# The start of a two-layer conditioned transformer kernel, rewritten: group 0 in halves, K placed from PSUM, films on ScalarE and GpSimd, weights loaded late

## What is computed

```python
# layer 0
tp = silu(cond) @ Wt + bt          # six vectors: shift, scale, gate (attention), shift, scale, gate (MLP)
h = layernorm(x) * (1 + scale_msa) + shift_msa
h = attention(h, Wqkv, Wproj)      # 16 heads of 8, softmax over the 32 rows of a sequence
x = x + gate_msa * h
h = layernorm(x) * (1 + scale_mlp) + shift_mlp
x = x + gate_mlp * (gelu(h @ W1 + b1) @ W2 + b2)
# layer 1
h = film(rmsnorm(x), cond, film1)  # x * (1 + scale) + shift, both from cond @ w + b
x = x + softmax(Q K^T / sqrt(D)) V @ proj + proj_b     # one head of 128
h = film(rmsnorm(x), cond, film2)
x = x + gelu(h @ mlp_w1 + b) @ mlp_w2 + b
```

## Time and profile before

| | us |
|---|---|
| median of 3 runs | 259.19 (258.96 to 259.65) |
| the profiled execution | 258.97 |
| its span in the trace | 257.1 |
| TensorE busy | 236.4 |
| VectorE busy | 163.9 |
| ScalarE busy | 154.9 |
| GpSimd busy | 151.1 |

### The profile page before, as it was taken

The page is one execution under the profiler, slowest core; times in us unless marked ns, Lnnn a source line. Parts: engine busy times, 40 slices in busy tenths (PEclk is TensorE's granted clock), DMA queues, the critical chain, the costliest instruction groups (busy, mean ns, idle before and its releaser), DMA issues.

```text
span 257.1 us, 9816 instructions
## 1 busy us (share of the span) xinstructions
PE 236.4 (92%) x3696; PEld 176.7 (69%) x3696; DVE 163.9 (64%) x510; ACT 154.9 (60%) x394; POOL 151.1 (59%) x161
## 2 busy tenths in 40 slices
PE   0588878999999998999999999999999999999995
PEld 0556556868778775687766669767775666777775
DVE  4868997879999999374454455378888444542002
ACT  2368566658668658925566545888757665444440
POOL 7442543855857768776666766797783545553110
PEclk9999999999999999999999999999999999999999
DMA  6964324443433443340000000000000011101112
GB/s 214 311 244 110 101 72 107 108 126 109 115 118 114 126 122 97 112 147 1 3 0 0 0 0 0 1 3 4 0 3 3 0 45 42 41 1 40 41 43 82
DMA packets 17451, 18.01 MB, mean 70 GB/s; under 512 B 2320, under 2 KB 13072, under 8 KB 17296
## 3 DMA queue, kind: packets, MB, share of 16 engines
q1 hardware_dynamic: 16848, 15.67, 21.6%
q10 hardware_dynamic: 576, 1.98, 2.3%
HBM read 11.48 MB, written 4.59 MB: 63 GB/s over the span
## 4 chain that ended last, share of the span: by engine, by line
PE 77%; DVE 7%; issue 5%; ACT 3%; POOL 3%; DMA 3%; SPq 1%; ACTq 0%; POOLq 0%; DVEq 0%
PE bank L1146 22%; PE bank L962 10%; PE pair L962 10%; PE bank L938 5%; PE bank L1036 5%; PE pair L1006 4%; PE bank L1057 3%; PE bank L1018 2%; PE pair L1159 2%; PE bank L1153 2%; PE bank L1184 2%; ACT xhat L770 2%; PE bank L1006 2%; DMA X<-x 2%; PE bank L986 2%
## 5 line engine op out<-in xcount | busy, mean ns | idle before, releaser
L770 ACT ACTIVATE xhat<-X,shift,rstd 128x128 f32 (+1 forms) x96 | 40.3, 486 | 50.7 <-POOL shift L332 50.6
L1146 PE MATMUL bank<-W,Kx 128*128 128x128 f32 x512 | 59.6, 275 | 0.0
L1146 PEld LDWEIGHTS bank<-W,Kx 128*128 128x128 f32 x512 | 58.5, 192 | 1.0 <-issue 1.0
L343 POOL TENSOR_TENSOR h<-hA,B 128x512 f32<-128x512 f32 x32 | 33.6, 1049 | 34.4 <-DVE hA L505 34.1
L505 DVE TENSOR_TENSOR hA<-bank,A 128x512 f32<-128x512 f32 x32 | 21.8, 681 | 32.3 <-PE bank L938 17.0
L962 PE MATMUL bank<-h,W 128*128 128x512 f32 x62 | 32.0, 597 | 0.1
L351 POOL TENSOR_TENSOR Ss<-Sc,smax 128x512 f32<-128x512 f32 x16 | 16.8, 1051 | 25.9 <-DVE smax L531 25.9
L330 POOL TENSOR_TENSOR rstd<-v_sb,minus_half 128x4 f32<-128x4 f32 x24 | 24.6, 1026 | 11.6 <-DVE v_sb L490 6.5
L962 PE MATMUL pair<-h,W 128*128 128x512 f32 x62 | 29.4, 592 | 0.0
L938 PEld LDWEIGHTS bank<-ident,xhat 128*128 128x128 f32 x128 | 15.9, 146 | 16.6 <-issue 12.2
L825 ACT ACTIVATE Kx<-bank,col 128x512 f32<-128x512 f32 x32 | 21.7, 678 | 8.1 <-PE bank L962 8.1
(11 more groups left out here) (132 smaller groups left out, 452.0 us busy)
## 6 DMA issues: line engine op xcount, KB each, us to landing
values_scratch<-Vs SPq DMA_DIRECT2D x8, 288.0 KB, 2.2
Vx<-values_scratch SPq DMA_DIRECT2D x32, 72.0 KB, 2.1
gate<-gates_scratch SPq DMA_DIRECT2D x32, 64.0 KB, 2.2
gate<-gates_scratch SPq DMA_DIRECT2D x16, 128.0 KB, 2.6
out<-X SPq DMA_DIRECT2D x7, 256.0 KB, 2.3
Kx<-Ks SPq DMA_DIRECT2D x24, 64.0 KB, 1.9
W<-weights ACTq DMA_DIRECT2D x1, 1152.5 KB, 6.2
X<-x SPq DMA_DIRECT2D x4, 256.0 KB, 6.8
```

The lines of the kernel that those rows point to most:

```text
L343: pool.tensor_tensor(by_seq(h[:, p, :]), by_seq(hA[:, p, :]), B[:, seqs(gg)].unsqueeze(2).broadcast_to([P, GB, L]), ALU.add).then_inc(h_re ...
L770: last = act.activation(xhat[:, p, P * t:P * (t + 1)], X[:, x_tile(gg, t), :], ACT.Identity, bias=shift[:, p, t:t + 1], scale=rstd[:, p, t ...
L1146: last = pe.matmul(y[t // 2][:, P * t:P * (t + 1)], gT[:, p, n, P * t:P * (t + 1)], w(f"W2_{phase // 2}", n), start=(n == 0), stop=(n == N ...
```

## The change

Weights are laid out anew (`Wqkv` right behind `Wt`, layer 1's V weight stored transposed, `v1T`), and the loads are split and moved: `Wt` in two pieces around the rows of group 1, `Wqkv` alone from ScalarE's queue, then the films and projections. The rest of `x` (groups 4 to 7) is loaded behind the first spread of V. The MLP weights of layer 0 are loaded in group 5 of attention 0, those of layer 1 in the first group of MLP 0.

```diff
@@ sync
-            lo, hi = W_AT["Wt"][0], W_AT["Wproj"][0]
-            sp.dma_start(W[:, lo:hi], weights[:, lo:hi]).then_inc(wt_in, 16)
-            for g in range(1, 4):
+            lo, mid, hi = W_AT["Wt"][0], W_AT["Wt"][0] + 2 * D, W_AT["Wqkv"][0]
+            sp.dma_start(W[:, lo:mid], weights[:, lo:mid]).then_inc(wt01_in, 16)
+            sp.dma_start(X[:, TG:2 * TG, :], xv[:, TG:2 * TG, :]).then_inc(x_in[1], 16)
+            sp.dma_start(W[:, mid:hi], weights[:, mid:hi]).then_inc(wt_in, 16)
+            for g in range(2, 4):
                 sp.dma_start(X[:, TG * g:TG * (g + 1), :], xv[:, TG * g:TG * (g + 1), :]).then_inc(x_in[g], 16)
-            sp.dma_start(X[:, 4 * TG:, :], xv[:, 4 * TG:, :]).then_inc(x_in[4], 16)
...
                 sp.dma_start(values_d[p], Vs[:, p, :]).then_inc(v_stored[p], 16)
+                if g == 1:
+                    store_gates()
                 sp.wait_ge(v_stored[p], 16 * (g // 2 + 1))
...
-            sp.wait_ge(gate_ready, 1)
-            for b in range(TB):
-                sp.dma_start(gates_d[b].rearrange("i t d -> t i d"),
-                             gate_b[b:NB:TB, :].rearrange("t (i d) -> t i d", i=2)).then_inc(gates_stored, 16)
-            sp.wait_ge(zeros_ready, 1)
+            sp.wait_ge(zeros_ready, 2)
             spread_v(0, 0)
-            sp.wait_ge(gates_stored, 16 * TB)
-            spread_gates(0, 0, NG)
+            sp.dma_start(X[:, 4 * TG:, :], xv[:, 4 * TG:, :]).then_inc(x_in[4], 16)
             for g in range(1, NG):
                 spread_v(g, g % 2)
                 if g < NG - 1:
                     spread_k(g + 1, (g + 1) % 2)
+                if g == 1:
+                    sp.wait_ge(gates_stored, 16 * TB)
+                    spread_gates(0, 0, NG)
...
@@ scalar
+                if isinstance(g, int) and g == NG - 3:
+                    lo, hi = W_AT["W1_0"][0], W_AT["W1_1"][0]
+                    act.dma_start(W[:, lo:hi], weights[:, lo:hi]).then_inc(wmlp_in, 16)
...
+                        lo = W_AT["W1_1"][0]
+                        act.dma_start(W[:, lo:], weights[:, lo:]).then_inc(wmlp1_in, 16)
```

```diff
@@ vector
+            def place_k_low(half):
+                dve.wait_ge(k2_ready, half + 1)
+                at, k_ps = slice(GN // 2 * half, GN // 2 * (half + 1)), bank[5][:, GN // 2:GN] if half == 0 else bank[6][:, 0:GN // 2]
                 for r in (0, 1):
-                    last = dve.tensor_scalar(Kx[:, g, r, :], Ks[:, g, :], r_mask[:, r:r + 1], None, ALU.mult)
+                    last = dve.tensor_scalar(Kx[:, 0, r, at], k_ps, c("bk"), r_mask[:, r:r + 1], ALU.add, ALU.mult)
                 last.then_inc(k_placed, 1)
+            def apply_first(gg):
+                dve.wait_ge(pool_chain, gg + 2)
+                for t in range(TG):
+                    last = dve.tensor_scalar(xhat[:, gg, P * t:P * (t + 1)], X[:, x_tile(gg, t), :].rearrange("p t d -> p (t d)"),
+                                             mk[:, gg, t:t + 1], rstd[:, gg, t:t + 1], ALU.add, ALU.mult)
...
+            apply_first(0)
+            modulate_half(0)
+            dve.tensor_tensor(B[:, 0:NB], bank[5][:, 0:NB], t_mul[:, :], ALU.add).then_inc(ab_ready, 1)
+            modulate_half(1)
@@ scalar
+            def place_k_high(half):
+                for r in (2, 3):
+                    last = act.activation(Kx[:, 0, r, at], bank[3][:, at], ACT.Identity, bias=r_bias[:, r:r + 1],
+                                          scale=r_mask[:, r:r + 1])
@@ gpsimd
+            pool.tensor_tensor(gate_b[:, :], xg[:, 0, 2 * NB:4 * NB], row[:, 0:2, :].rearrange("p i d -> p (i d)"),
+                               ALU.add).then_inc(gate_ready, 1)
+            film0_rest()
             add_shift(1, 1)
+            subtract_max(0, 0)
             power(2, 0)
@@ tensor
+            for n in range(24):
+                pe.transpose(bank[7][:, 0:P], ident[:, :], ident[:, :])
...
+            pe.wait_ge(ab_ready, 1)
+            first_qk(0)
+            values0(0, 0)
...
+            scores0(0, 0)
+            rows_T(1, 1)
+            first_qk(1)
+            film1()
+            keys0(1, 1)
```

More of the change, by code:

```diff
@@ new lines, in _ @@
+            link(last)
+            dve.tensor_scalar(ag0[:, :], c("g1"), one_plus[:, 0:1], None, ALU.mult)
+            dve.tensor_scalar(ab0[:, :], c("be1"), one_plus[:, 0:1], c("bt", 0), ALU.mult, ALU.add).then_inc(cols_ready, 1)
+            dve.wait_ge(exp_c, 1)
+            link(dve.tensor_tensor(sT[:, :], eT[:, :], kind[:, 0, 2 * NG:2 * NG + 1].broadcast_to([D, NB]), ALU.add))
+            link(dve.reciprocal(eT[:, :], sT[:, :]))
+            first_stats(0)
+            dve.tensor_tensor(sT[:, :], cT[:, :], eT[:, :], ALU.mult).then_inc(y_used, 1)
@@ L689, in attention0 @@
+                update(0, g - 1, 1 - p)
                 aggregate(g + 4, p, True)
@@ L1102, in attention0 @@
                     pe.wait_ge(wmlp_in, 16)
-                if first:
-                    fold(0)
                 pe.wait_ge(v_spread[p], 16 * HQ * (k + 1))
@@ L1111, in attention0 @@
                 scores_T(g, 1)
-                if first:
-                    fold(1)
-                    pe.wait_ge(ab_ready, 3)
-                elif not last:
+                if not last:
                     project0(g - 1, 1 - p)
```

367 lines of the change are left out of this document (227 added, 140 removed).

## The result

The changed kernel takes **263.21 us** (median of 6 runs, 261.93 to 265.29); the kernel before, run on the same chip, takes 259.80 us (6 runs, 258.96 to 262.59). The ratio is 1.0141, with a 95% interval of 1.0105 to 1.0177. The change makes the kernel slower, by more than the range of the prediction allows. The profiled execution took 262.90 us, with a span of 261.1 against the 257.1 us of before.

The account below looks back on a forecast made before the run. From 60 us TensorE alone was taken to set the pace; before it VectorE was full from 20 to 40, behind the first group's latency chain. Forecast: 258.97 - 2.5 (start, after SyncE's queue) + 0.1 (weights) = 256.6 us, range 253.6 to 259.4.

Parts of the forecast that it names:

- Part 1: The first group up to its scores: first scores at 13.0 us, 5.8 before 18.83.
- Part 2: From first scores to the loop, on a full VectorE: entry at 29.6 us, 5.0 earlier, bounds 28.4 and 31.2.
- part 4: Weights moved to group 5 and the first MLP group: 0.1 us lost; late rest of X and turned V weight free.
- Part 3: SyncE's queue up to the keys of group 3: gives back gain, take-up at 48.0 instead of 50.47, 2.5 us won.
- SyncE's queue takes over: Longest row at each queue step: keys of group 3 land at 51.7, 1.2 later than before; 260.2 us, chance 0.13.
- Ports: VectorE's normalisation of group 1 meets GpSimd's gate and film operations: 1.6 us more on VectorE, 258.2 us, chance 0.13.
- Weights in the way: The load in group 5 delays V or K of the next groups: 2.6 us lost, 259.1 us, chance 0.12.
- TensorE's pace: SyncE keeps its medians, so TensorE reaches the keys of group 3 at 45.0: gain 5.4, 253.6 us, chance 0.20.

Follow-up runs that it names:

- experiment 6: Changed kernel with gates stored and first spread around V of group 0, without the 24 transposes of ident; 259.33 us, ratio 0.9980 to the kernel before.
- experiment 1: Changed kernel with the rest of x issued at the start again; 262.96 us, ratio 1.0112 to the kernel before.
- kernel 2: Changed kernel with the gates stored and first spread around V of group 0; 257.58 us, ratio 0.9887 to the kernel before.
- kernel 8: Changed kernel with gates stored and first spread around V of group 0, and gates spread two groups at a time; 257.05 us, ratio 0.9853.
- experiment 9: Changed kernel with only the gates spread two groups at a time, stores and first spread left late; 259.00 us, ratio 0.9963 to the kernel before.
- experiment 12: Kernel before with only the changed kernel's order of gate stores and spreads on SyncE; 263.95 us, ratio 1.0111 to the kernel before.
- kernel 3: Changed kernel with the rest of x at the start and gates stored and first spread around V of group 0; 256.63 us, ratio 0.9832.
- 5: Changed kernel with only the four gate stores moved behind V of group 0; 265.90 us, ratio 1.0169 to the kernel before.
- experiment 7: Changed kernel with gates stored and first spread around V of group 0, and both MLP weight loads behind the first film; 256.63 us, ratio 0.9816.
- 10: Changed kernel with gates spread two groups at a time and the rest of x at the start; 258.70 us, ratio 0.9910 to the kernel before.
- kernel 11: Changed kernel with x at the start, gates stored and first spread around V of group 0, spread two groups at a time; 255.46 us, ratio 0.9830.

## Why the prediction was wrong, step by step

**Part 1 was right.** Forecast 13.0 for the first scores, measured 13.77, within the 12.4 to 13.8 named. The terms that were off: four normalised tiles on VectorE took 1.11 us (0.28 each, not 0.2), and film 0 ended at 9.9 instead of 9.3, for which hA waited 0.60. The 24 transposes of ident took 5.32 us, to 8.3 instead of about 7.9; that the short durations hold behind them was right, and experiment 6 shows that they hold because of them.

**Part 2 failed in the changed kernel, and its sum was right.** Forecast 29.6 for the entry, bounds 28.4 to 31.2; measured 35.66. Without the late megabyte it is 30.74 (experiment 1), so the counting of VectorE's work was within 1.1 us. An entry after 31.2 was named as what would make the forecast wrong. The failed sentence is the one in part 4 that "the late rest of X (1 MB, issued near 18, used at 28) and the turned V weight (...) cost nothing, covered by part 2's VectorE work". I asked of a moved transfer only whether its own reader would wait for it: it landed at 25.9, in time. I didn't ask whom it stands beside. Moving it back takes away a stop of 1.74 us and, behind that, 2.3 us of half clock; 0.5 of the 4.9 us lies ahead of the stop already (the scores from 24.28 instead of 24.75). The late megabyte does not always do this: kernels 2, 8 and 9 have it too and enter at 31.86, 31.87 and 32.34, with stops of 0.77 to 1.29 and no half clock behind them.

**Part 3 was wrong by its choice of durations, and this is what decided the sign.** The mechanism was the one named: a queue that gives back the gain. It put the keys of group 3 at 48.0, 2.5 us earlier than before; they are taken up at 53.35, and at 51.30 in experiment 1. Here are its steps, forecast (medians, with the reserve apart) and measured. The column of experiment 1 is the fair one for part 3, since there the loop is entered almost when forecast.

| step of SyncE's queue | forecast | changed | exp. 1 | exp. 12 |
|---|---|---|---|---|
| V of group 1 stored at | 25.0 | 26.07 | 25.59 | 27.42 |
| four gate stores | 2.6 | 2.59 | 3.31 | 3.41 |
| four spreads of V | 1.7 | 2.77 | 2.01 | 2.03 |
| K of group 2 from | 29.7 | 33.92 | 31.45 | 34.21 |
| its four spreads | 2.4 (+0.9) | 2.42 | 3.10 | 3.60 |
| eight gate spreads and a landing | 5.2 (+1.2) | 6.58 | 6.47 | 6.13 |
| V of group 2 stored, landed | 2.2 (+0.5) | 2.17 | 3.01 | 2.67 |
| four spreads of V | 1.7 | 3.07 | 1.74 | 3.02 |
| four spreads of K | 2.4 | 2.38 | 2.38 | 2.38 |
| end of these to take-up | 1.3 (+0.5) | 2.57 | 2.91 | 2.09 |
| keys of group 3 taken up at | 48.0 | 53.35 | 51.30 | 54.34 |

The eight gate issues took what I had reserved for them, 6.1 to 6.6. But steps with little or no reserve were long too: in one trace or another the stores of the gates by 0.7, a group's spreads of V by 1.1 and 1.4, and from the last issue of K to the take-up by 0.8 to 1.6. Each trace has several steps at their medians and several well over, and apart from the gates they are not the same ones. Adding the medians of ten steps, with a reserve on four of them, understates such a chain.

The trace of the kernel before had this already. Its groups of four spreads of V took 1.74 to 2.54 us, its groups of four gate spreads up to 90 us took 1.83 to 3.03: the sums of four single medians, 1.7 each, lie below the shortest group of four. And the last step was read from the median of all landings of K, while the keys of group 3 themselves, issued by 47.29 and taken up at 50.47, took 3.18 us there, against 1.3 with 0.5 in reserve (landings of the four transfers from 44.91, kernel before):

```profile
DMA to landing us min/median/max: 1.8/2.1/3.6
```

The longest row, 3.6, which the prediction named for K and mostly left out, belongs to this very transfer.

In the changed kernel there is one wait more, between the spreads of V, done at 31.86, and K of group 2 at 33.92: its keys had to be computed at half clock first. I gave the row "with the longest row at each step", 51.7, a chance of 0.13, against it "nearly every step must be long". Experiment 1 ended at 51.30 with only some of them long.

**And the wait has a tail that no case of mine had.** A wait of 2 to 3 us was priced at its length, and the clock behind it at nothing, without a reason. In the changed kernel and in the profiled runs of 1, 3, 5, 7, 10 and 12 the granted clock falls around it. That is 1.1 us more in the changed kernel; in experiment 12 it is 263.5 - 54.34 = 209.2 from the take-up to the end against 206.6 before, 2.6 us, in a run that is 1.3 over the median of its ten. In kernel 2, with three waits of 1.1 to 1.25, the clock stays at 1.00.

**The sum**, remade with what was measured: 258.97 + 2.9 (keys of group 3 later than before, instead of 2.5 earlier) + 1.1 (what the stretch behind them grew by, with 3 us of half clock in it) = 263.0, measured 262.90. It closes by construction, since the two terms are the profiled span cut at the take-up; what it shows is their sizes. The 0.1 for the weights is not to be seen in the trace.

**The rivals.** *SyncE's queue takes over* is what happened, at a take-up of 53.35 beyond its 51.7; its price of 260.2 was short by the late entry and by the clock. *Ports*: the four normalised tiles of group 1, beside GpSimd's gate and film operations, took 1.53 us together instead of 0.8. That is 0.7, less than the 1.6 of the rival, and experiment 1 entered at 30.74 with it inside. The four of group 0, with GpSimd idle or in one operation of 0.20 beside them, took 1.11, so some 0.4 is left for a meeting with GpSimd. The prediction cites the Trainium skill, "SBUF — State Buffer", section "Who interferes with whom", for a VectorE tensor_scalar and a GpSimd instruction that shut each other out for a whole instruction. These 0.4 us beside 1.3 us of GpSimd's work agree with it in direction and are far from a full exclusion. *Weights in the way*: no wait in group 5, so its 2.6 us are excluded; experiment 7 shows that putting the loads back wins nothing that could be told. *TensorE's pace* needed SyncE's medians; no kernel here reached it, and the best one took up the keys at 45.93.

**What stays open.** The stop itself. In every kernel with the new start that has it between 25 and 29 us in the score products, it cuts the same run of them, without a releaser: 1.74 us in the changed kernel, 0.77, 2.67, 0.77 and 1.29 in kernels 2, 5, 8 and 9, all with the rest of x late, and 0.62 in kernel 3, with x early. It is absent in 1, 10 and 11, with x early, and in 7, with x late. Kernel 6 has none in the scores but one of 1.11 at 30, in the weighing. The kernel before has two such stops of 0.8, at 37 and 41, with no megabyte near. A fetch of TensorE's instructions that travels in the same transfer engines would fit: short when they are free, long beside a megabyte. The transfer view of the changed kernel between 23 and 26 us, while x is arriving, has one packet of such a kind (queue and kind: packets, MB, share of 16 engines):

```profile
q1 hardware_dynamic: 313, 0.61, 68.8%
q8 instruction: 1, 0.02, 2.5%
```

That is argued, not shown: whose instructions they are the trace doesn't say. What the one profiled execution of each shows is that in the changed kernel the stop is there and with x moved back it isn't. Also, in four pairs of kernels (the changed one against 1, 2 against 3, 9 against 10, 8 against 11) the late x has the higher ratio each time, by 0.2 to 0.6%, none of them beyond its intervals. Nor do the runs say how the doubled spread and the tail of the clock share the 1.8% of experiment 9, since the tail goes with the wait.

The second open end is the last step for the keys of group 3. With one spread of gates, or none, between K and V of group 2, the time from the end of their issues to the take-up is 1.4 us in the profiled executions of kernels 2, 6, 9 and 11 and 3.0, 2.85 and 2.7 in those of 3, 7 and 10, and the clock fell in these three and not in the other four. That may be what parts the executions of 256 us from those of 260 in kernel 3. What makes the transfer short or long no run here shows.

## What to carry to other kernels

When a queue between two engines gets new instructions, count the instructions and the landings that stand ahead of the next needed transfer, not the bytes: four spreads of 128 KB took 1.97 us where eight of 64 KB with a landing between them took 6.58 (though the next four of 128 KB took 3.53). Take the time of a group of issues from the trace as a group, and the landing from the transfer that is waited for. Price a chain of ten queued steps well above the sum of its medians, look at the case in which some of them are long as the likely one, and add to a long wait of TensorE a tail for the clock behind it. And a transfer that is moved off a quiet place has to be checked against everything that runs beside its new place, even when its own reader has time.

## What of the hardware was not expected

- The clock fell behind short idle times. With TensorE idle for 1.74 us, and for 1.43 and 2.78, the granted clock was 0.50 from 29 to 36 and from 53 to 56 in the changed kernel, and K on 512 columns took 2.08 instead of 1.02 us; in experiment 12, idle for 1.5 and 2.29, it was 0.51 from 53 to 60. In kernels 2 and 11, with waits of up to 1.25 and 1.65 us, it stayed at 1.00, and so it did in kernel 6, with one of 1.70: a single wait's length doesn't decide it. The mean granted clock over the span is on record for every execution. In the two kernels that spread over 4 us it goes with the time: in kernel 3 the three of 255.86 to 256.63 us have 1.000 and those of 259.87 and 260.29 have 0.987; in kernel 7 the three of up to 257.12 have 1.000 and the one of 259.99 has 0.987; all six of kernel 11 have 1.000. Smaller differences it does not order: kernel 2 took 257.71 at 0.993 and 257.72 at 1.000.
- At the start of the program the granted clock reads 1.00, but the durations are those of the lower level: in kernel 6 K on 256 columns took 1.06 us, half of the 2.08 that 512 columns took at a granted clock of 0.50. Behind the 24 transposes it took 0.59 to 0.67.
- A store of 288 KB that is issued while a megabyte is arriving landed after 5.0 us instead of 2.2 (kernel 2; 4.0 in kernel 8), and what reads it back waited for all of that.
